# An attention stage on one core: the last unit's sums of a window are issued behind the first score slice of the next turn

## The reference, cut to what matters

```python
def _transformer_conv(x, src, dst, wq, bq, wk, bk, wv, bv, ws, bs):
    q = (x @ wq + bq).reshape(n, H, C); k = ...; v = ...
    alpha = einsum('ehc,ehc->eh', q[dst], k[src]) / sqrt(C)
    amax = segment_max(alpha, dst)
    ex = exp(alpha - amax[dst])
    denom = segment_sum(ex, dst)
    a = ex / (denom[dst] + 1e-16)
    out = segment_sum(a[:, :, None] * v[src], dst).mean(axis=1)
    return out + x @ ws + bs
```

## Time and profile before

| | |
|---|---|
| median of 3 runs | 5511.68 us (5506.94 to 5514.25) |
| profiled execution, its own time | 5511.28 us |
| span of that execution | 5509.6 us |
| attention, windows of layer 1 (3148 to 3740 us) | 592 us, PE busy 536.34 us |
| attention, windows of layer 2 (3813 to 4405 us) | 592 us, PE busy 537.79 us |

### The profile page before, as it was taken

How to read it: one execution, slowest core, us unless ns; L and a number is a source line. 1 busy time by engine, 2 the same in 40 slices (tenths; PEclk the granted TensorE clock), 3 DMA queues, 4 the chain that set the end, 5 groups by cost and what they waited for, 6 DMA issues and landing times. The chain is left out here.

```text
span 5509.6 us, 107131 instructions
## 1 busy us (share of the span) xinstructions
PE 3854.9 (70%) x31278; PEld 2925.4 (53%) x31283; DVE 3861.6 (70%) x9964; ACT 2078.9 (38%) x2842; POOL 1418.6 (26%) x1703
## 2 busy tenths in 40 slices
PE   4666668743444554444545699998999879988997
PEld 2222248643444444444444455554555559986996
DVE  7999967656565556566563377774777778877887
ACT  2433334000111111111111256654556657765785
POOL 0000000006777777777777100000000000000000
PEclk8999989865555555555555699997999969997998
DMA  1111125532222222222212122211222121102111
GB/s 39 59 67 64 59 102 219 215 114 57 59 60 59 54 60 60 58 60 59 60 47 50 40 70 71 71 54 45 70 71 71 42 74 47 48 30 79 48 48 30
DMA packets 235224, 370.68 MB, mean 67 GB/s; under 512 B 169839, under 2 KB 175973, under 8 KB 235142
## 3 DMA queue, kind: packets, MB, share of 16 engines
q1 hardware_dynamic: 190006, 264.11, 14.8%
q0 software_dynamic: 41536, 85.08, 6.0%
q10 hardware_dynamic: 3600, 20.48, 0.9%
HBM read 292.58 MB, written 76.99 MB: 67 GB/s over the span
## 5 line engine op out<-in xcount | busy, mean ns | idle before, releaser
L1069 POOL DMA_INDIRECT en_got<-edge_q,en_now x1296 | 1306.1, 1008 | 409.2 <-issue 324.4
L1258 PE MATMUL en_t<-ident,en_got 128*128 128x128 f32 x1296 | 361.2, 434 | 959.4 <-DVE en_got L1152 959.4
L1296 ACT ACTIVATE en_hid<-en_t 128x512 f32<-128x512 f32 x324 | 193.5, 597 | 1651.0 <-DMA en_got<-edge_q,en_now 1409.4
L1258 PEld LDWEIGHTS en_t<-ident,en_got 128*128 128x128 f32 x1296 | 231.6, 217 | 1037.8 <-DVE en_got L1152 1037.8
L1266 PEld LDWEIGHTS en_o<-en_w2s,en_hid 128*128 128x128 f32 x2592 | 582.7, 333 | 0.0
L1266 PE MATMUL en_o<-en_w2s,en_hid 128*128 128x64 f32 x2592 | 577.4, 411 | 0.0
L1152 DVE TENSOR_TENSOR en_got<-en_got,p (+1 forms) x324 | 224.4, 693 | 496.3 <-ACTq L1290 463.6
L456 PE MATMUL cnt_ps<-cnt_hot_l,cnt_hot_k 128*128 128x400 bf16 x1600 | 360.2, 357 | 193.1 <-DVE cnt_hot_l L421 177.2
L1849 PE MATMUL r1s_ps<-hp,r1s_bits 128*128 128x193 bf16 x5000 | 423.1, 248 | 26.5 <-DVE r1s_bits L1802 13.6
L1849 PE MATMUL r0s_ps<-hp,r0s_bits 128*128 128x193 bf16 x5000 | 422.6, 247 | 26.5 <-DVE r0s_bits L1802 13.5
L1849 PEld LDWEIGHTS r1s_ps<-hp,r1s_bits 128*128 128x128 bf16 x5000 | 417.8, 98 | 31.8 <-issue 31.4
(11 more groups left out here) (389 smaller groups left out, 7399.8 us busy)
## 6 DMA issues: line engine op xcount, KB each, us to landing
en_got<-edge_q,en_now POOLq DMA_INDIRECT x1296
count_panels<-cnt_panel SPq DMA_DIRECT2D x25, 800.0 KB, 3.4
type_panels<-cnt_panel SPq DMA_DIRECT2D x25, 800.0 KB, 4.8
c0s_panel<-count_panels SPq DMA_DIRECT2D x25, 800.0 KB, 4.3
count_rows<-c0s_rows ACTq DMA_DIRECT2D x25, 800.0 KB, 3.5
c1s_panel<-count_panels SPq DMA_DIRECT2D x25, 800.0 KB, 6.0
c1s_rows<-count_rows SPq DMA_DIRECT2D x25, 800.0 KB, 7.5
en_raw<-count_panels SPq DMA_DIRECT2D x25, 800.0 KB
```

What stands on the lines that cost most here:

```text
L1069: pool.indirect_dma_start(out=got[:, i, j, :], out_offset=None, in_=k.q[:, :], in_offset=bass.IndirectOffsetOnAxis(ap=now[i][:, j:j + 1], ...
L1258: last = pe.transpose(tps[i % 2][:, j * P:(j + 1) * P], got[:, i, j, :], k.ident[:, :])
L1296: act.activation(hid[i % 2][:, :], tps[i % 2][:, :], ACT.Relu).then_inc(lined, 1)
```

## The change

The sums of unit 12 are no longer issued at the end of their window. In the next window they are issued between slice 0 and slice 1 of the scores. Window 24, the last, computes no further scores: there the sums of unit 12 of window 23 stand at its start. Those of window 24 stand behind the loop. Nothing is added or removed.

```diff
                 if more:
                     score(w + 1, 1 - u, 0)
+                if not (isinstance(w, int) and w == 0):
+                    sum_up(w - 1, 1 - u, NU - 1)
+                if more:
                     score(w + 1, 1 - u, 1)
                 for j in range(NU):
                     turn(w, u, j)
...
                     if more and j in NEXT:
                         score(w + 1, 1 - u, NEXT[j])
-                sum_up(w, u, NU - 1)
             windows(pe, window)
+            sum_up(W - 1, (W - 1) % 2, NU - 1)
             wait_alone(pe, outed, W + 2, passed_e)
             pe.transpose(tps[1][:, 0:P], out_t[:, :], k.ident[:, :]).then_inc(backed, 1)
```

## The result

The changed kernel takes 5517.47 us (median of 14 runs, 5510.52 to 5523.60) against 5507.43 us for the kernel before in the same session: a ratio of 1.0016, 95% interval 1.0009 to 1.0024. It is slower by some 9 us (8.8 by the ratio, 10.0 between the medians), and the upper end of the interval lies past 0.2%. The forecast was +3.7 us on the median then known, 5515 us with a range of 5508 to 5522. The median lies in it, but less than half of the loss was foreseen.

The account below looks back on a forecast made before the run. PE at the full clock was taken to bound the windows, through sums 11 to turn 6, then ACT and DVE. 22 x 0.07 + 24 x 0.09 = +3.7 us gave 5515.4, rounded to 5515 us; range 5508 to 5522.

Parts of the forecast that it names:

- the 41.0 us: PE's wait, 25 times, for ACT's copy ahead of sums 11; said to stay, as the moved sums wait for nothing.
- two switches: PE changing between slices and sums once more each way: sums 11 to turn 0 takes 3.08 us, not 2.73; 0.35 us more.
- the wait for veil 0: Slice 2's wait on PE for DVE, 0.21 or 0.20 us; said to go, net +0.07 us at boundaries without a branch.
- the way over ACT: Sums 12 over take_out, exp and line 0 to sums 0: 3.54 us against PE's 3.67, so it holds; rival's chance 0.05.
- The unit prices: PE times, start to next start: 8 sum records 0.59 us, a slice up to the turn 1.06, 4 sum records alone 0.37.
- The rival of the loads that run ahead: Weight loads of sums 12 and slice 1 run early on PE, both switches go: -10 us, 5501.5 us; chance 0.07.
- the circle: What sets the window's period: PE from sums 11 to turn 6, then ACT and DVE; PE delays there lengthen the period.
- the branch: Loop branch exposes 0.34 us ahead of slice 0, taken as unchanged: slice 2 at 4.01 us against 3.92, +0.09 us each.
- the full clock: PE in both attention stretches taken at granted share 1.00, the 2.4 GHz level, busy 536.34 of 592 us.
- The rival of the branch that holds slice 0: At boundaries with a branch slice 0 stays at 1.15 us after sums 11: 5.3 us more, 5520.5 us; chance 0.13.

Follow-up runs that it names:

- the slice in the idle time: The kernel before, with slice 0 moved between turn 12 and sums 11, sums of unit 12 left in place: 5468.15 us, ratio 0.9930.
- each half of the change: Kernel before, sums of unit 12 moved only into windows 1, 3, ... 23: 5504.35 us, ratio 1.0000; only into windows 2, 4, ... 24: 5510.05 us, ratio 1.0005.
- the added matmul: Kernel before, one 128x128 matmul added behind sums 0 of each second window: 5521.14 us, ratio 1.0037; the same in the changed kernel: 5519.81 us, ratio 1.0025.

## Why the prediction was right or wrong

*Right: what waits, and for what.* That the 41.0 us belong to sums 11 and stay (39.7 us after), that the branch-free boundary gains two switches and loses the wait for veil 0, +0.07 us, and that the way over ACT holds by a little. The unit prices came out to the hundredth: 1.06 us for slice 0 with sums behind it (3384.86 - 3383.80), 0.37 us for four records alone. The way over ACT had 0.22 us to spare (3412.66 - 3412.33, less 0.11), where I had 0.13. The rival of the loads that run ahead did not appear: the loads of sums 12 stood idle for 0.76 us and began in the same hundredth as their matmuls.

```profile
3384.86 0.20 PEld L1538 LDWEIGHTS a0s_o<-a0s_ext,va 128*64 128x64 f32 x4 [0.76 <-issue]
```

The Trainium skill (TensorE: Matmul & The Clock Gate, Step-by-step: what each phase is for) has loads pulled ahead of running matmuls where the row groups don't conflict or where they go to the background buffer. This row shows none of it for loads of 128 rows behind a slice; which of the two conditions was missing no run shows.

*Right: the circle.* Layer 2's periods grew by 0.07 and 0.02 us, what PE's part of the circle grew by (0.06 and 0.03 us in the timelines above), and the slice in the idle time took 38 us off.

*A little off: the branch.* I kept its 0.34 us whole; slice 0 starts 0.87 us after sums 11, not 0.93. Of the branch 0.28 us is exposed (0.87 - 0.59) where a wait and four records fewer stand ahead of it; that these are the reason no run shows. +0.03 us in place of +0.09, 1.4 us less in all: 2.3 us for the order in place of 3.7.

*Wrong: the full clock.* The step that failed stands in the first part: PE "at the full clock (granted share 1.00)". That share was read as a constant, and no term of the sum and no rival had the clock in it. It had been 1.00 only by rounding, and only in layer 1; layer 2 had 0.99. In the 1184 us of both layers there were three stretches of 3.4 us at 0.50, two of them at the layers' starts and one at a boundary (4026.9 us); and each window has 1.6 to 1.7 us of idle PE, every second one with the branch's gap behind it. The missing term is four further stretches of 1.5 us. The rival of the branch that holds slice 0 would have given just these 9 us, and the range was stretched for it, but it did not happen: slice 0 moved up by 0.28 us. So the time lies in the range for a reason that I did not have, and that is luck. There is a second piece of it: the base of 5511.68 us, a median of three, lay 4.3 us above that of 14 runs, and without it the forecast would have missed the 5517.47 us by 6 us and not by 2.5.

*What stays open.* Filling the idle time removes the stretches, lengthening the window in the old order brings them, and each half of the change brings few. That fits the place in time at which boundaries fall, but no run shows it directly. It does not exclude that the new order helps as well, since the added matmul lengthens the pair by 0.21 us and the change by 0.10, and no run had one with the other held. The numbers of stretches come from two profiles of each of the two kernels and from one of every other. Nor can I say beforehand which boundary will be hit.

## What to carry to other kernels

In a loop that leaves PE idle for 1.7 us once in 24 us the clock is not a constant of the stage: look for stretches at the lower level in several profiles before a change of a few hundredths of a microsecond a window is priced, and fill the gap with work that is needed. Before moving work past a wait, find which instruction of a merged row waits: here the 1.7 us belonged to the sums ahead of the ones moved, and the same slice put in front of that wait gave 0.7%.

## What the runs showed of the hardware that I had not expected

- Single stretches of 3.4 us at a granted clock of 0.50 come in a stage where PE is over 90% busy (536.34 of 592 us). In both kernels they began within 0.3 us of the start of sums 11 or 1.7 to 1.9 us behind it, but for those in a layer's last window, often at two boundaries in a row, and cost 1.3 to 1.6 us each. With three idle-time matmuls whose output nobody reads there were none in the one profile of either kernel, and the kernel before with them is no slower (ratio 0.9996).
- One float32 matmul of 128x128, 0.11 us of records, costs 0.21 us of the period with a slice behind it (24.21 against 24.00 us), and nothing ahead of turn_back (24.01 us).
